# Routing a mixture of experts on one Trainium2 core: scatters by slot, or a token list made by matmuls and gathers

## The chip, the cores and the metric

The kernel runs on one core of a Trainium2 chip. The metric is device time in microseconds (us), the median of several executions. In the profile PE is TensorE (PEld its weight loads), DVE is VectorE, ACT is ScalarE, POOL is GpSimdE and SP is SyncE, which here only issues DMAs.

## The reference, cut to what matters

Two layers act on x, 32 batches of 128 tokens of 128 values (4096 tokens). Each layer is a cross attention with 16 heads over a context, then a mixture of 8 experts. All results are added to x with a tanh gate. The text calls them layer 1 and layer 2; the code has `layer == 0` and `layer == 1`.

```python
x = x + tanh(g_xattn[0]) * xattn0(layernorm(x), ctx)
x = x + tanh(g_ffn[0])   * ffn0(layernorm(x))
x = x + tanh(g_xattn[1]) * xattn1(layernorm(x), ctx)
x = x + tanh(g_ffn[1])   * ffn1(layernorm(x))

def ffn0(x):   # 8 experts, width 256, each expert picks its cap = 4096 / 8 = 512 best tokens
    probs = softmax(xt @ Wg)
    top_idx = top_k(probs.T, cap)                  # per expert
    masked = where(selected, probs.T, -inf)
    tok2exp = where(assigned, argmax(masked), argmax(probs.T))   # one expert a token
    return probs[tok2exp] * (gelu(x @ W1[tok2exp]) @ W2[tok2exp])

def ffn1(x):   # 8 experts, width 512, each token picks its two best, weights normalised to 1
```

## The kernel before, in words

Each layer has two stages. The **attention stage** (`pair_slots`) walks over 16 pairs of batches in software-pipelined slots: in slot p statistics are taken of pair p+4, it is transposed and projected as p+3, its queries and keys are written to DRAM and read back in another layout by SP (p+3, p+2), row maxima are found as p+1, scores and exponentials as p, values and output as p-1 and p-2. At the end, pair p-2 gets the statistics of the norm before the experts, and as p-3 its normed rows go to N and its router logits to LG. GpSimdE makes each reciprocal root (L445, L446 for the attention's norm, L466 to L469 for the experts'). Slots run from p = -4, so that the first pairs' statistics stand at the very start of the stage. The order of the work is written by hand, engine by engine, and each engine executes its own list in order.

The **expert stage** of layer 1 begins on DVE (`expert_layer`, L1210). `route_by_experts` (L1162) finds for each expert the 512th largest probability by a search on the bits of the float. It has ROUNDS = 15 rounds of BITS = 2 bits. A round (L1172 to L1184) counts for each of three candidates how many of 256 values per partition are at or above it (L1174, three counts with an accumulator), lets a matmul with SAME sum the counts over the partitions (L808), compares with 512, and takes the largest candidate that passed as the prefix of the next three. Then masks, two rank steps (`ranks`, L1087) and a choice of the best expert give each token a slot: expert e has a region of its own in DRAM, and the token takes the next free row of it (`slot_of`, L1096; `fill` adds the token's number and weight to its row of N).

GpSimdE scatters N to the DRAM tensor `dispatched` by 32 indirect DMAs, one for each batch (`dispatch`, L478; L494). Meanwhile DVE makes the tables of the tiles (`tables`, L1102): which rows and which expert each of TILES = 23 tiles of 256 slots has. SP waits for all scatters and reads the tiles, three buffers deep (L379 on). For each tile TensorE transposes it (L640), multiplies with the first matrices (L834), ScalarE applies Gelu (L615), TensorE multiplies with the second (L844), DVE scales by the tokens' weights (L1262), and GpSimdE scatters the result to `returned` in token order by two indirect DMAs of 128 rows (L504). After the last scatter SP reads it all back in four parts (L406), and DVE adds each to x with the gate (`combine`, L1268), one part at the head of each of the first four slots of layer 2's attention (`first_layer_result`, L1282).

Layer 2 routes during its attention, in groups of batches (`choose`, L885), scatters both choices of each token from GpSimdE's slots, and then has 39 tiles in the same manner. That part of the kernel keeps its form.

## Time and profile before

| | us |
|---|---|
| median of 3 runs | 791.73 (791.7 to 794.16) |
| the profiled execution, its time | 792.8 |
| the profiled execution, its span in the trace | 791.0 |
| busy in the span: PE, PEld | 539.4, 435.0 |
| busy in the span: DVE, ACT, POOL | 506.0, 346.8, 309.4 |
| mean granted TensorE clock | 0.847 of full |

The span is the time from the first to the last instruction of the trace. The stages lie in it about so: attention of layer 1 to 215 us, search and routing to 270, scatters to 312, tiles to 383, attention of layer 2 to about 590, its tiles to the end. A share of busy time is a mean over these stages, so it doesn't say what bounds one of them. PEclk is the clock that TensorE was granted, where 1.0 is 2.4 GHz and 0.5 is 1.2 GHz.

### The profile page before, as it was taken

To read this page: it belongs to the slowest core of one execution; us is meant where nothing else is said; L and a number is where in the kernel's file an instruction comes from. 1 tells how busy PE (TensorE), PEld (TensorE's weight loads), DVE (VectorE), ACT (ScalarE), POOL (GpSimd) and SP (SyncE) were. 2 spreads that over 40 slices of the span, in tenths; PEclk is the share of its full clock that TensorE was granted. 3 is DMA by queue.
4 is the path that set the end of the run, shared out by engine and by line. 5 is a ranking of instruction groups with operands and counts; after the bars stand their busy time and mean duration, and the time that the engine had idled before them with its cause. 6 is when DMAs were issued, how large, how long until landed. Compare 5 with 4: busy or idle time off the path is not lost.

```text
span 791.0 us, 17073 instructions
## 1 busy us (share of the span) xinstructions
PE 539.4 (68%) x5502; PEld 435.0 (55%) x5502; DVE 506.0 (64%) x1666; ACT 346.8 (44%) x798; POOL 309.4 (39%) x438
## 2 busy tenths in 40 slices
PE   1689999998511000988179999898710999999950
PEld 0467777776300000777156666675410899999940
DVE  4679888986287800344278999998662456655625
ACT  0256777777400000433026777675710555555510
POOL 6212233311200275477311224564775254554540
PEclk9979999999755555899559999999955899999985
DMA  8553332320000032233434555442113222222219
GB/s 270 149 179 97 97 93 85 92 83 4 1 0 0 18 106 62 75 108 101 129 115 144 167 161 162 138 131 76 37 49 107 59 72 76 73 72 72 69 56 297
DMA packets 97703, 76.71 MB, mean 97 GB/s; under 512 B 12880, under 2 KB 91600, under 8 KB 97168
## 3 DMA queue, kind: packets, MB, share of 16 engines
q1 hardware_dynamic: 89504, 57.27, 25.6%
q0 software_dynamic: 7040, 14.63, 5.5%
q10 hardware_dynamic: 1072, 3.73, 1.4%
q8 instruction: 46, 0.75, 0.4%
q14 instruction: 41, 0.34, 0.1%
HBM read 45.76 MB, written 33.62 MB: 100 GB/s over the span
## 4 chain that ended last, share of the span: by engine, by line
PE 46%; DVE 17%; issue 10%; POOL 9%; DMA 7%; ACT 5%; SPq 4%; ACTq 1%; DVEq 0%; POOLq 0%
PE bank L834 9%; PE bank L844 9%; PE bank L640 6%; PE bank L666 5%; PE bank L787 5%; POOL dispatched L479 4%; PE bank L654 4%; POOL returned L504 4%; DVE MX L979 4%; DVE PT L1174 2%; ACT OT L588 2%; PE bank L711 1%; PE bank L742 1%; PE bank L713 1%; PE bank L700 1%
## 5 line engine op out<-in xcount | busy, mean ns | idle before, releaser
L533 ACT ACTIVATE PT<-bank 128x512 f32<-128x512 f32 x256 | 151.9, 597 | 92.3 <-PE bank L654 91.5
L979 DVE TENSOR_REDUCE MX<-bank 128x4 f32<-128x512 f32 x256 | 172.8, 681 | 28.3 <-PE bank L666 26.1
L504 POOL DMA_INDIRECT returned<-PT,META_ROW x124 | 118.9, 959 | 113.4 <-DVE PT L1262 89.1
L479 POOL DMA_INDIRECT dispatched<-N,SLOT x96 | 94.7, 986 | 97.5 <-DVE EX L1217 57.4
L666 PE MATMUL bank<-KS,QS_N 96*128 96x128 f16 x1024 | 104.2, 227 | 11.7 <-DMA KS<-spread 7.2
L610 ACT ACTIVATE XGT<-bank 128x256 f32<-128x256 f32 x62 | 23.8, 383 | 191.7 <-PE bank L640 191.7
L844 PEld LDWEIGHTS bank<-WALL,HT 128*128 128x128 f32 x808 | 100.7, 195 | 7.3 <-issue 4.1
L844 PE MATMUL bank<-WALL,HT 128*128 x808 | 102.6, 279 | 1.6 <-ACT HT L615 0.8
L834 PE MATMUL bank<-XGT,XT_HL_WR 128*128 128x256 f32 x404 | 102.4, 394 | 0.0
L654 PE MATMUL bank<-QS_N,KS 98*128 98x512 f16 x256 | 98.1, 389 | 3.3 <-DMA QS_N<-MH 3.2
L666 PEld LDWEIGHTS bank<-KS,QS_N 96*128 96x128 f16 x1024 | 77.5, 103 | 35.9 <-DMA KS<-spread 9.4
L640 PE MATMUL bank<-CONST,PT 128*128 128x128 f32 x124 | 26.3, 296 | 82.8 <-issue 76.1
L834 PEld LDWEIGHTS bank<-XGT,XT_HL_WR 128*128 128x128 f32 x404 | 75.2, 199 | 8.0
L621 ACT ACTIVATE HT<-bank,XT_HL_WR 128x256 f32<-128x256 f32 x156 | 63.9, 471 | 21.4 <-PE bank L834 21.4
L787 PE MATMUL bank<-PT,VA 128*32 128x128 f32 x2048 | 70.6, 280 | 0.1
L640 PEld LDWEIGHTS bank<-CONST,PT 128*128 128x128 f32 x124 | 15.7, 151 | 87.3 <-issue 77.0
L787 PEld LDWEIGHTS bank<-PT,VA 128*32 128x32 f32 x2048 | 53.1, 111 | 18.0 <-issue 11.0
L466 POOL TENSOR_SCALAR MINUS<-MV_N 128x2 f32<-128x2 f32 x32 | 7.5, 233 | 127.4 <-DVE MV_N L883 127.2
L1258 DVE TENSOR_TENSOR PT<-bank,WALL 128x256 f32<-128x256 f32 x39 | 16.6, 425 | 43.9 <-PE bank L844 36.0
L1232 DVE COPY XT_HL_WR<-WALL 128x516 f32 (+1 forms) x62 | 23.7, 382 | 29.9 <-issue 19.6
L445 POOL TENSOR_SCALAR VE<-MV 128x2 f32<-128x2 f32 x32 | 7.0, 220 | 88.8 <-DVE MV L883 88.6
L1239 DVE CAST META_ROW<-PT 128x2 int32<-128x2 f32 x23 | 4.1, 177 | 56.9 <-DMA PT<-dispatched 35.5
(198 smaller groups left out, 890.5 us busy)
## 6 DMA issues: line engine op xcount, KB each, us to landing
spread<-XT_HL_WR SPq DMA_DIRECT2D x96, 128.0 KB
PT<-dispatched SPq DMA_DIRECT2D x62, 132.0 KB, 2.1
QS_N<-spread SPq DMA_DIRECT2D x128, 48.0 KB
KS<-spread SPq DMA_DIRECT2D x32, 192.0 KB
WALL<-in_w SPq DMA_DIRECT2D x8, 578.0 KB
CT<-in_ctx SPq DMA_DIRECT2D x32, 128.0 KB, 3.0
dispatched<-in_pads SPq DMA_DIRECT2D x2, 1056.0 KB
dispatched<-in_pads SPq DMA_DIRECT2D x16, 132.0 KB
```

Of the source, the lines that this page charges most:

```text
L479: pool.indirect_dma_start(xs[layer][:, :], bass.IndirectOffsetOnAxis(ap=SLOT[:, k, b:b + 1], axis=0), N[:, b, :], None).then_inc(scattered ...
L504: pool.indirect_dma_start(ys[layer][:, :], bass.IndirectOffsetOnAxis(ap=META_ROW[:, a.f, c:c + 1], axis=0), YS[:, a.f, c, :], None).then_i ...
L533: nc.scalar.activation(PT[:, c, 4 * g:4 * g + 4, :].rearrange("p j q -> p (j q)"), ST[i % 2][:, :], ACT.Exp, scale=SCALE[layer]).then_inc( ...
L610: nc.scalar.activation(XGT[:, a.u, :], bank[4 + a.u][:, 0:TILE], ACT.Copy).then_inc(xg_kept, 1)
L621: last = nc.scalar.activation(HT[:, a.u, m, :], bank[2 * a.u + m // 2][:, TILE * (m % 2):TILE * (m % 2) + TILE], ACT.Gelu, bias=WR[:, a.t, ...
L640: return nc.tensor.transpose(to, of, ident[0:n, 0:n])
L654: nc.tensor.matmul(ST[i % 2][:, :].rearrange("p (j q) -> p j q", j=J), KS[0:98, x.r, g, c * P:(c + 1) * P], QS[0:98, x.r, J * g:J * g + J, ...
L666: last = nc.tensor.matmul(MB[i % 2][:, j * P:(j + 1) * P], QS[0:96, m.r, J * g + j, c * P:(c + 1) * P], KS[0:96, m.r, g, c * P:(c + 1) * P ...
L787: last = nc.tensor.matmul(PA[32 * g:32 * g + 32, 256 * c + P * (j // 2):256 * c + P * (j // 2) + P], VA[:, b.r, c, head(g, j), :], PT[:, c ...
L834: last = nc.tensor.matmul(bank[2 * a.u + m // 2][:, TILE * (m % 2):TILE * (m % 2) + TILE], WR[:, a.t, m * P:(m + 1) * P], XGT[:, a.u, :], ...
L844: last = nc.tensor.matmul(bank[6 + a.u][:, c * D:(c + 1) * D], HT[:, a.u, m, c * P:(c + 1) * P], WALL[:, bass.ds(r + (W1COLS[layer] + m * ...
L979: V.tensor_reduce(out=MX[:, m.u, 2 * J * g + c:2 * J * (g + 1):2], in_=MB[i % 2][:, :].rearrange("p (j k) -> p j k", j=J), op=ALU.max, axi ...
```

## The change

**Search.** The candidates become whole numbers held as floats: the bits of the probabilities are cut to their high 14 bits for 8 rounds, then to the low 16 for 7 rounds. DVE makes two of the three counts and ScalarE the third, as a sum of signs, whose limit is 2 * 512 - 4096. The number of candidates that pass (an accumulator) times a step, plus a part worked out beforehand (PRE), gives the next three.

**Token list.** A slot is now a place in the row of all tiles (expert's first tile * 256 + rank), so that slot s lies in block s / 128 at place s % 128. OWN (128 tokens x 32 batches x 46 blocks) marks each token's block, POS its place. IDS is OWN times the token's partition (ScalarE) and OWN times its batch (GpSimdE). 32 matmuls of POS with IDS sum the partition and the batch of the token at each place of each block: LIST. The normed rows were stored plainly to DRAM (`normed`) by SP during the attention, and GpSimdE gathers two blocks for each tile, 46 gathers, in place of the 32 scatters and SP's reads.

**Results.** They aren't weighted and stay in slot order: DVE copies them, SP stores each tile plainly. In layer 2's attention GpSimdE gathers each batch's 128 rows by SLOT, 32 gathers, and DVE adds them to x with weight * gate (W0) for each pair before its statistics. The four combines are gone. Half of the tables, the tokens' numbers and weights in their rows, and some masking operations go; `starts` (the tiles' starts) now stands before the slots.

```diff
@@ route_by_experts, DVE
-                for t in range(ROUNDS):
-                    for m in range(CANDS):
-                        last = V.tensor_scalar(out=HITS[:, m, :], in0=PRT[:, :], scalar1=CAND[:, m:m + 1].bitcast(F32),
+                bits = PF[:, 0:B * E].bitcast(I32)
+                link(V.tensor_scalar(out=BITS_I[:, :], in0=bits, scalar1=((1 << 30) - 1) ^ low_mask, scalar2=None, op0=ALU.bitwise_and))
+                V.tensor_copy(PRT[:, :], BITS_I[:, :]).then_inc(candidates, 1)
+                dve.wait_ge(candidates, 2)
+                for t in range(ROUNDS):
+                    for m in range(CANDS - 1):
+                        last = V.tensor_scalar(out=HITS[:, m, :], in0=PRT[:, :], scalar1=CAND[:, m:m + 1],
                                                scalar2=None, op0=ALU.is_ge, op1=ALU.add, accum_out=COUNT[:, m:m + 1])
                     last.then_inc(mask_ready, 1)
+                    link(V.scalar_tensor_tensor(out=PRE[:, :], in0=sign, scalar=CAND[:, 0:1], in1=delta[:, t, :], op0=ALU.mult, op1=ALU.add))
+                    if t == 0:
+                        V.tensor_scalar(out=LOW_I[:, :], in0=bits, scalar1=low_mask, scalar2=None, op0=ALU.bitwise_and).then_inc(lows_cut, 1)
                     dve.wait_ge(counted, t + 2)
-                    link(V.scalar_tensor_tensor(out=BEST[:, 0:CANDS], in0=PO[:, 0:CANDS], scalar=float(CAP),
-                                                in1=CAND[:, :].bitcast(F32), op0=ALU.is_ge, op1=ALU.mult))
-                    if t < ROUNDS - 1:
-                        reduce(best, BEST[:, :], ALU.max)
-                        tt(CAND[:, :], best.bitcast(I32).broadcast_to([P, CANDS]), digit[:, t + 1, :], ALU.bitwise_or)
+                    link(V.scalar_tensor_tensor(out=PASSED[:, :], in0=PO[:, 0:CANDS], scalar=1.0, in1=limit, op0=ALU.mult, op1=ALU.is_ge,
+                                                accum_out=NPASS[:, :]))
+                    found = V.scalar_tensor_tensor(out=CAND[:, :], in0=step[:, t, :], scalar=NPASS[:, :], in1=PRE[:, :],
+                                                   op0=ALU.mult, op1=ALU.add)
...
@@ expert_layer, ScalarE
+                    for t in range(ROUNDS):
+                        act.wait_ge(candidates, t + 2)
+                        act.wait_ge(counted, t + 1)
+                        nc.scalar.activation(HITS[:, CANDS - 1, :], PRT[:, :], ACT.Sign, bias=CAND[:, CANDS - 1:CANDS],
+                                             accum_out=COUNT[:, CANDS - 1:CANDS]).then_inc(counted_act, 1)
...
+                    act.wait_ge(own, 1)
+                    nc.scalar.activation(IDS[:, :, 0, :], OWN[:, :, :], ACT.Copy, scale=const("partition")).then_inc(ids_p, 1)
@@ list_tokens, DVE (new)
+                V.tensor_tensor(out=OWN[:, :, :], in0=const("blocks").unsqueeze(1).broadcast_to([P, B, BLOCKS]),
+                                in1=sm[4].unsqueeze(2).broadcast_to([P, B, BLOCKS]), op=ALU.is_equal).then_inc(own, 1)
+                for k in range(4):
+                    V.tensor_tensor(out=POS[:, part * k:part * (k + 1), :], in0=const("places").unsqueeze(1).broadcast_to([P, part, P]),
+                                    in1=sm[5][:, part * k:part * (k + 1)].unsqueeze(2).broadcast_to([P, part, P]),
+                                    op=ALU.is_equal).then_inc(positions, 1)
...
+                dve.wait_ge(listed, 1)
+                link(V.tensor_copy(FIRST_IDS[:, :], PA[:, 0:BLOCKS]))
+                V.scalar_tensor_tensor(out=LIST[:, :], in0=PA[:, BLOCKS:2 * BLOCKS], scalar=float(P), in1=FIRST_IDS[:, :],
+                                       op0=ALU.mult, op1=ALU.add).then_inc(list_ready, 1)
@@ expert_layer, TensorE
+                    pe.wait_ge(ids_p, 1)
+                    pe.wait_ge(ids_b, 1)
+                    for b in range(B):
+                        if b % (B // 4) == 0:
+                            pe.wait_ge(positions, 4 * b // B + 1)
+                        last = nc.tensor.matmul(PA[:, 0:2 * BLOCKS], POS[:, b, :], IDS[:, b, :, :].rearrange("p k n -> p (k n)"),
+                                                start=(b == 0), stop=(b == B - 1))
@@ GpSimdE
-                if layer == 0:
-                    pool.wait_ge(copied, 1)
-                    for b in range(B):
-                        dispatch(0, 0, b)
+            def first_experts():
+                pool.wait_ge(own, 1)
+                nc.gpsimd.tensor_tensor(out=IDS[:, :, 1, :], in0=OWN[:, :, :], in1=const("batch").unsqueeze(2).broadcast_to([P, B, BLOCKS]),
+                                        op=ALU.mult).then_inc(ids_b, 1)
+                pool.wait_ge(normed_kept, 16 * PAIRS)
+                pool.wait_ge(list_ready, 1)
+                for i in range(TILES[0]):
+                    a = Tile(0, i)
+                    if a.g >= 3:
+                        pool.wait_ge(xg_t, a.g - 2)
+                    for c in range(2):
+                        pool.indirect_dma_start(XG[:, a.t, c, 0:D], None, normed[:, :],
+                                                bass.IndirectOffsetOnAxis(ap=LIST[:, 2 * i + c:2 * i + c + 1], axis=0)).then_inc(XA[a.t], 16)
+                for r in range(4):
+                    pool.wait_ge(SO[r], 16 * len(range(r, TILES[0], 4)))
+                gather_results(Pair(1, 0, 0))
@@ attention_slot, GpSimdE, after RSTD of pair p + 4
+                    if layer == 1:
+                        for k in range(2 * p + 9, min(2 * p + 11, PAIRS)):
+                            gather_results(Pair(1, k // 4, k % 4))
+            def gather_results(g):
+                if g.p >= 8:
+                    pool.wait_ge(combined, g.p - 7)
+                for c in range(2):
+                    pool.indirect_dma_start(YG[:, g.p % 8, c, :], None, ys[0][:, :],
+                                            bass.IndirectOffsetOnAxis(ap=SLOT[:, 0, g.b + c:g.b + c + 1], axis=0)).then_inc(YGS[g.p % 8], 16)
@@ attention_slot, SP, at the end of a slot (y = pair p - 3)
+                if (y := pair(-3)) and y.g < PAIRS:
+                    sp.wait_ge(n_copied, y.g + 1)
+                    sp.dma_start(normed[y.b * P:(y.b + 2) * P, :].rearrange("(c p) d -> p c d", p=P),
+                                 N[:, y.b:y.b + 2, 0:D]).then_inc(normed_kept, 16)
@@ attention_slot, DVE, before the statistics of n = pair p + 4
+                    if n and layer == 1:
+                        dve.wait_ge(YGS[n.p % 8], 32 * (n.p // 8 + 1))
+                        for c in range(2):
+                            last = V.scalar_tensor_tensor(out=batch(n, c), in0=YG[:, n.p % 8, c, :], scalar=W0[:, n.b + c:n.b + c + 1],
+                                                          in1=batch(n, c), op0=ALU.mult, op1=ALU.add)
+                        last.then_inc(combined, 1)
```

At digit 8 (`t + 1 == HIGH`) DVE also keeps the high digits, adds the low bits to what is left of the values, and loads the low candidates: a copy, a scaled sum over 256 values, a copy. The constants grow from 905 to 1214 columns of 128 values, since the tables of the search and of the list are among them.

## Rows read from the trace of the kernel before

**Rows 1.** Shares of the chain that ended last, whole kernel, by engine (page, part 4).
```profile
PE 46%; DVE 17%; issue 10%; POOL 9%; DMA 7%; ACT 5%; SPq 4%; ACTq 1%; DVEq 0%; POOLq 0%
```

**Rows 2.** Stretch 270 to 300 us: length, busy of PE, PEld, DVE, ACT, POOL, PEclk, DMA share, GB/s.
```profile
270.00:300.00 30.00, 0.00 (x0) 0.00 (x0) 6.59 (x27) 0.00 (x0) 22.99 (x24) 0.50 0.29 88
```

**Rows 3.** Timeline, from the search's end to the first scatter: start us, us, engine, line, operation.
```profile
252.46 0.61 DVE L1065 TENSOR_TENSOR RA<-PR,THR 128x256 f32<-128x256 f32 x1
...
268.36 0.18 DVE L1100 CAST SLOT<-SM 128x32 int32<-128x32 f32 x1
...
269.73 1.22 POOL L479 DMA_INDIRECT dispatched<-N,SLOT  x1 [57.45 <-DVE EX L1217]
```

**Rows 4.** The first stage's last scatter in the chain of waits: start us, us to landing.
```profile
309.22 2.26 DMA dispatched<-N,SLOT
```

**Rows 5.** Timeline of TensorE's work on tiles: three rows at 1.2 GHz, two at 2.4 GHz.
```profile
314.46 0.66 PE L640 MATMUL bank<-CONST,PT 128*128 128x128 f32 x2 [49.51 <-issue]
...
316.01 1.92 PE L834 MATMUL bank<-XGT,XT_HL_WR 128*128 128x256 f32 x4
...
320.89 2.07 PE L844 MATMUL bank<-WALL,HT 128*128 x8 [0.83 <-ACT HT L615]
...
329.64 1.03 PE L834 MATMUL bank<-XGT,XT_HL_WR 128*128 128x256 f32 x4
...
330.50 1.05 PE L844 MATMUL bank<-WALL,HT 128*128 x8
```

**Rows 6.** GpSimdE in 323.8 to 384.3 us, groups by line: busy us, mean ns, idle before.
```profile
L504 POOL DMA_INDIRECT returned<-PT,META_ROW x46 | 44.3, 962 | 28.5 <-DVE PT L1262 16.3 <-issue 12.2
```

**Rows 7.** Timeline of the end of the first expert stage and the start of layer 2.
```profile
377.81 0.61 DVE L1262 TENSOR_SCALAR PT<-bank,META_W 128x128 f32<-128x128 f32 x2 [1.20 <-PE bank L844]
...
389.89 0.29 DVE L880 BATCH_NORM_STATS2 STATS<-X 128x6 f32<-128x128 f32 x1
...
391.05 0.72 POOL L446 TENSOR_TENSOR RSTD<-VE,EXPO 128x2 f32<-128x2 f32 x1
...
393.64 0.29 DVE L880 BATCH_NORM_STATS2 STATS<-X 128x6 f32<-128x128 f32 x1
...
396.07 0.68 DVE L1029 TENSOR_TENSOR XT_HL_WR<-bank,XT_HL_WR 128x512 f16<-128x512 f32 x1
...
399.88 0.60 DVE L1014 TENSOR_SCALAR XN<-X,MV,RSTD 128x128 f32<-128x128 f32 x2 [1.13 <-POOL RSTD L446]
```

**Rows 8.** One 9 us slot of layer 2's attention, columns as in rows 2.
```profile
464.00:473.00 9.00, 8.56 (x121) 6.43 (x120) 8.75 (x30) 6.71 (x16) 2.28 (x6) 1.00 0.60 172
```

**Rows 9.** Timeline of one round of the search, and the start of the next.
```profile
221.96 0.48 DVE L1174 TENSOR_SCALAR_CACHE_REDUCE PT<-PT,CAND 128x256 f32<-128x256 f32 x1
...
223.16 0.09 DVE L1174 DVE_READ_ACCUMULATOR PT<-PT,CAND 128x1 bf16 x1
...
223.53 0.16 DVE L1178 SCALAR_TENSOR_TENSOR BEST<-bank,CAND 128x3 f32<-128x3 f32 x1 [0.28 <-PE bank L808]
...
224.11 0.48 DVE L1174 TENSOR_SCALAR_CACHE_REDUCE PT<-PT,CAND 128x256 f32<-128x256 f32 x1
```

**Rows 10.** Timeline: ScalarE's pass over 256 values, the Exp before the search.
```profile
216.59 0.42 ACT L604 ACTIVATE PR<-PR 128x256 f32<-128x256 f32 x1 [0.94 <-DVE PR L1150]
```

**Rows 11.** Timeline: ScalarE's change of function table in the first expert stage.
```profile
318.01 1.28 ACT L615 ACT_TABLE_LOAD   x1 [1.37 <-PE bank L834]
```

**Rows 12.** DVE over 256 values, groups by line with shapes, 214 to 270 us.
```profile
L1065 DVE TENSOR_TENSOR RK<-RK,bank 128x256 f32<-128x256 f32 x4 | 1.7, 421 | 0.1
```

**Rows 13.** GpSimdE's sum over 256 values, one line's instructions: ns least/median/most.
```profile
L451 POOL TENSOR_TENSOR X<-X,BIAS x16: 721/723/731, 18.1 to 156.0; 128x256 f32<-128x256 f32 x16
```

**Rows 14.** Four 128-column matmuls at the low clock, in the chain of waits.
```profile
403.13 0.61 PE bank L666 x4
```

**Rows 15.** DVE's scaled sum over 256 values, groups by line, 396 to 600 us.
```profile
L1042 DVE SCALAR_TENSOR_TENSOR X<-OK,GATES,X 128x256 f32<-128x256 f32 x16 | 7.6, 477 | 0.0
```

**Rows 16.** DMA issues by line: KB each, us from issue to landing.
```profile
CONST<-in_const SPq DMA_DIRECT2D x1, 452.5 KB, 3.4
```

More of the change, by code:

```diff
@@ L39, with search_tables @@
 CANDS = 2 ** BITS - 1
+HIGH = 8
 ROUNDS = 30 // BITS
+LOW_BITS = BITS * (ROUNDS - HIGH)
 GROUPS = ((0, 3), (3, 3), (6, 3), (9, 3), (12, 2), (14, 2))
 NB = 6
+def search_tables():
+    sign = np.ones(CANDS)
+    sign[-1] = -1
+    digit, step = np.zeros((ROUNDS + 2, CANDS)), np.zeros((ROUNDS, CANDS))
+    first, delta = np.zeros((2, CANDS)), np.zeros((ROUNDS, CANDS))
+    for phase, (t0, t1, unit) in enumerate(((0, HIGH, 2 ** LOW_BITS), (HIGH, ROUNDS, 1))):
+        half = np.zeros(CANDS)
+        half[-1] = unit / 2
+        here = [unit * 4.0 ** (t1 - 1 - t) * np.arange(1, CANDS + 1) - half for t in range(t0, t1)] + [np.zeros(CANDS)]
+        first[phase] = sign * here[0]
+        for t in range(t0, t1):
+            step[t] = sign * unit * 4.0 ** (t1 - 1 - t)
+            delta[t] = sign * (here[t - t0 + 1] - here[t - t0][0])
+    limit = np.full(CANDS, float(CAP))
+    limit[-1] = 2 * CAP - T
+    return sign, limit, first, step, delta
 def constants():
+    sign, limit, first, step, delta = search_tables()
     p = np.arange(P)[:, None]
@@ L63, in constants @@
         ("place", 2 * p + np.arange(2)[None, :]),
+        ("places", one * np.arange(P)[None, :]),
+        ("blocks", one * np.arange(BLOCKS)[None, :]),
+        ("batch", one * np.arange(B)[None, :]),
+        ("partition", one * p),
+        ("search_sign", one * sign),
+        ("search_limit", one * limit),
+        ("search_first", one * first.reshape(1, -1)),
+        ("search_step", one * step.reshape(1, -1)),
+        ("search_delta", one * delta.reshape(1, -1)),
     ]
@@ L389, in expert_layer @@
-                for i in range(TILES[layer]):
-                    a = Tile(layer, i)
-                    if a.g >= 3:
-                        sp.wait_ge(xg_t, a.g - 2)
-                        sp.wait_ge(meta, a.g - 2)
+                sp.wait_ge(pads, 16 * (1 + E))
+                sp.wait_ge(scattered, 16 * B * 2)
+                for i in range(TILES[1]):
+                    a = Tile(1, i)
+                    sp.wait_ge(xg_t, a.g - 2)
+                    sp.wait_ge(meta, before(i - 2))
@@ new lines, in slot @@
+                        link(V.tensor_tensor(out=w2, in0=is_second, in1=row[:, :, D + 2], op=ALU.mult))
+                        V.tensor_tensor(out=META_W[:, a.f, :], in0=w1, in1=w2, op=ALU.add).then_inc(meta, 1)
+                    if (a := tile(-1)) and layer == 0:
+                        dve.wait_ge(y_done, a.g + 1)
+                        await_results(dve, a)
+                        V.tensor_copy(YS[:, a.f, :, :].rearrange("p c d -> p (c d)"), bank[6 + a.u][:, 0:2 * D]).then_inc(y_kept, 1)
@@ new lines, in slot @@
+                    if (a := tile(-1)) and layer == 1:
+                        dve.wait_ge(y_done, a.g + 1)
+                        dve.wait_ge(meta, a.i + 1)
+                        y = bank[6 + a.u][:, 0:2 * D].rearrange("p (c d) -> p c d", c=2)
+                        r = dve.value_load(TBL[0:1, 1, a.i:a.i + 1], min_val=0, max_val=(E - 1) * W)
+                        link(V.tensor_tensor(out=YS[:, a.f, :, :], in0=y,
+                                             in1=WALL[:, bass.ds(r + (W - D), D)].unsqueeze(1).broadcast_to([P, 2, D]), op=ALU.add))
```

323 lines of the change are left out of this document (174 added, 149 removed).

## The prediction

> **What bounds the kernel now.** The view to read first is the chain of waits, because the kernel is a series of stages and each has another limit. Over the whole kernel TensorE holds 46% of the chain, but DVE has 17% and GpSimdE 9% [rows 1], and the diff touches stages where these two decide. Next comes the table of stretches. From 270 to 300 us TensorE executes nothing and GpSimdE is busy for 22.99 of 30 us [rows 2]: this is the dispatch, 32 scatters in a line. The timeline gives its ends. The first operation after the search starts at 252.46, the slots are ready at 268.54, and the first scatter starts at 269.73 [rows 3]. The last starts at 309.22 and lands 2.26 us later [rows 4], and the first token tile reaches TensorE at 314.46 [rows 5]. Then the 23 tiles run at GpSimdE's pace: 46 scatters of 962 ns, with 0.30 us between two [rows 6], make 2.53 us a tile. TensorE at 2.4 GHz needs only 1.03 + 1.05 and about 0.4 for the transposes, 2.5 in sum but overlapped [rows 5]. The last result is scaled at 378.42, yet the statistics of layer 2 start at 389.89 [rows 7], because the scatter backlog, its landing, a read back and a combine lie between. In layer 2's attention one 9 us slot holds 8.75 us of DVE and 8.56 of TensorE work, and 2.28 of GpSimdE [rows 8].
>
> **The change, term by term.** The sum is made against the profiled execution, whose span is 791.0 us.
>
> *Search, -6.0 us.* A round lasts 2.15 us (221.96 to 224.11). It has three counts on DVE (1.29 us to the end of the last accumulator read), 0.28 of TensorE and its semaphores, and then three small operations of 0.16 with 0.03 between [rows 9]. After the change DVE makes two counts (1.29 less one pitch of 0.40: 0.89), TensorE keeps 0.28, and two small operations remain, the first with an accumulator read of the kind that takes 0.09: 0.16 + 0.09 + 0.16 and three gaps, 0.45. That is 1.62, or 0.53 saved, 8.0 over 15 rounds. The operation for PRE lies beside TensorE. ScalarE's count runs beside the two DVE counts. No row shows a ScalarE count with a sum; its nearest row is a plain pass over 256 values, 416 ns [rows 10]. Bounds are that 0.42 and twice a DVE count with its read, 1.1. I take 0.6, near the row, so it is covered by the 0.89. Against the 8.0 stand whole-number steps that are new: a mask and a cast before round 0 instead of one copy (+0.4), the low bits cut in round 0 (+0.35), the change from high to low digits (a copy, a scaled sum over 256 values, a copy, +0.85), and three small ones at the end (+0.4). Net -6.0, range -8.5 to +1.
>
> *A possible table load, 0.* ScalarE's change from Exp to Gelu shows a 1.28 us load after 1.37 idle [rows 11]; whether Sign needs one no row shows. Exp ends at 217.01 [rows 10] and the first round began 2.15 before 221.96, at 219.81 [rows 9]: 2.8 us in which a load can hide. Its bound is once 2.65. The Trainium skill, "ScalarE: Activation LUTs" (What ACT_TABLE_LOAD costs), has 1.28 us plus a drain of 1.38 for every switch to another set, which agrees with that row. By this rule, with the load behind the wait, the sum would be 2.65 us worse.
>
> *Routing after the search, -1.7 us.* It takes 15.9 us from 252.46 to the slots. An operation over 256 values takes 0.42 to 0.61, a small one 0.18 [rows 3, 12]. Removed: threshold copy 0.2, two casts of the mask 0.6, in each of two rank steps a copy and a subtraction (1.3), and of the masking a small one and two over 256 values (1.0): 3.1, each priced between these rows. Added: five to seven small operations for the tile starts, which stood behind the first scatter before, +1.4. Bounds -2.5 and -0.5.
>
> *Token list in place of the scatters, -30.6 us.* Before, 45.9 us lie between slots and first transposes (268.54 to 314.46). New, after the slots: three small operations 0.63; OWN over 1472 values, 1.75 by one value per 1.04 ns as the 256 in 0.42 imply [rows 12]. GpSimdE then multiplies 1472 values: 723 ns for 256 [rows 13] makes 3.3 (if 0.2 of it is start) to 4.2. DVE makes POS in the meantime (4 x 1.2 = 4.8), and 32 matmuls of 92 columns follow. Four of 128 columns took 0.61 with the clock low [rows 14], so 0.15 each, 4.8. GpSimdE's 3.4, then 4.8 and a gap: 8.3, bounds 6 and 11. Two reads of the bank 0.45, GpSimdE's wake 0.3. The list stands at slots + 11.4. Two gathers are issued (the second 1.5 later) and land: 2.3 as the scatter did [rows 4], bounds 1.8 and 4.2. First transposes at slots + 15.3.
>
> The port is a place where a rule speaks against the change. The GpSimdE sums of [rows 13] lie between 721 and 731 ns in all 16, so nothing held them up there. The Trainium skill, "SBUF — State Buffer" (SBUF: two separate sides), says that DVE with two SBUF inputs and GpSimdE exclude each other for a whole instruction. POS has two such inputs; by this rule its last quarter would end 3.2 us later and the list 0.7 later, the sum -35.5.
>
> *Tile stage, -1.7 us.* It lasts 64.0 us from first transposes to 378.42. New: GpSimdE issues 46 gathers instead of 46 scatters, each for the price of [rows 6], 44 steps x 1.265 = 55.7 from the first tile's rows to the last's, then a tile's way to its result, 6.35 as for the last tile before, and 0.3 for buffers in the cold start. 62.3. No row shows a gather's issue; the scatter's 0.96 is the nearest, both bounds 0.8 and 1.15, so -9 to +8 us for the stage. SP's stores are issued beside it.
>
> *Return, -4.7 us.* Before 11.5 us from 378.42 to 389.89. New: a store and its landing 2.3, wake 0.3, second gather's start 1.3, landing 2.3, two scaled sums of 0.3: 6.8. Bounds -6 and -1.
>
> *Front of layer 2, +3.5 us.* The new gathers stand between two pairs' reciprocal roots on GpSimdE, four to a slot, 5.05 us. In time from the first statistics (389.89), RSTD ends at 1.9 [rows 7]. The second pair's gathers land at 5.8, its statistics run at 6.4 instead of 3.75, and the low halves that DVE writes behind it (L1029) at 8.9 instead of 6.2: +2.7 for the first maxima. Pair three: RSTD is queued behind gathers until 13.5, XN at 14.5 instead of 10.0 [rows 7]. Part of that is hidden by slots that soon last 9 us [rows 8], longer than 5.05 + 0.9. Taken +3.5, bounds +2 and +8. The four old combines of 1.3 on DVE go.
>
> *DVE in layer 2, +4.5 us.* Twelve more pairs get two scaled sums over 128 values. One over 256 takes 477 ns [rows 15], so with their wait 0.55 a pair. While TensorE is the nearer limit part is hidden; with DVE at 8.75 of 9 [rows 8] all counts: half of six and all of six is 5.0, taken 4.5, bounds 2 and 6.6.
>
> *Start, +0.5 us.* The constants grow from 905 to 1214 columns, 154 KB more before anything may start; 452.5 KB landed in 3.4 us beside other loads [rows 16], so 0.5, bounds 0 and 1.2. SP gets 16 stores of N in layer 1's attention: issued at each slot's end, before SP waits for the next maxima in any case. 0, or +2 if their 2 MB slow the others.
>
> Sum -6.0 - 1.7 - 30.6 - 1.7 - 4.7 + 3.5 + 4.5 + 0.5 = -36.2. The profiled run took 792.8, that becomes 756.6; the median of the three runs is 1.07 lower, 791.73, so 755.5. Forecast 756.
>
> **Rivals.** *ScalarE's count is the longer branch.* For it: no row of a ScalarE sum. Against it: 0.42 against 0.89. If the pass takes 1.4, the rounds keep their 2.15 and 8 us are lost: 764. *Layer 2 pays double.* Gathers and roots share GpSimdE, 2 MB more are in flight where slots wait for DMAs, and every DVE operation counts: +16 instead of +8: 764. *Gathers land late.* Buffers are three, so a landing over about 5.5 us sets the pace. A scatter landed in 2.26 [rows 4], and the slowest landing in my rows is 3.4, the constants' among other loads [rows 16]. At 7 us a tile takes 3.0, +11, and each single gather's way costs 4.7 more, in list, return and front: 781.
>
> *TensorE stays at 1.2 GHz, and the kernel is slower.* Place: tile stage. TensorE idles before it and granted clock was 0.50 [rows 2]; at that clock a tile takes 0.66 + 1.92 + 2.07 = 4.65 [rows 5] against 2.53. Before, it rose between the rows of 320.89 and 329.64, with a backlog of landed rows; now rows come one tile at a time. For 23 tiles +48.8, so 805. It decides from 17 tiles on. Against it: at 1.2 GHz a tile needs longer than the feed gives, so TensorE is then never idle, and that went before the rise.
>
> *It doesn't do what it says*: only if the gathers had to wait for the 16 stores of N, and the search and 15.9 us of routing lie between. No chance of its own.
>
> **Chances.** Forecast 0.66 (own range 745 to 766), ScalarE 0.11, layer 2 double 0.12, late landing 0.06, low clock 0.05. The range 745 to 772 leaves out the last two and tails of the first. A change of 0.3% (2.4 us) is about what a measurement of this kernel can tell. Only the low clock isn't faster: faster 0.94, same 0.01, slower 0.05.
>
> **What would show it.** Rounds of 1.6 us with ScalarE's count ended before DVE's; 11.4 us from slots to list and 15.3 to the first transposes; 46 gathers at 1.26 in a line, none waiting for TensorE; 6.8 us from last result to statistics; third pair's XN 14.5 after the first statistics; DVE without idle time in layer 2. I am wrong if the tile stage isn't at GpSimdE's pace or if the front loses over 8 us.

## The result, and the profile after

The changed kernel takes 761.6 us (median of 4 runs, 757.79 to 766.54), the kernel before 791.72 beside it (4 runs, 790.95 to 794.16). The ratio is 0.962, with a 95% interval of 0.956 to 0.968: 30.1 us less. The forecast was 756 in a range of 745 to 772.

The profiled executions are 760.45 us (span 758.6) and 792.8 (span 791.0), 32.4 us apart. First, the chain that ended last by engine, which answers to [rows 1].

```profile
PE 41%; DVE 22%; issue 11%; POOL 10%; DMA 8%; ACT 5%; SPq 2%; ACTq 1%; POOLq 0%; DVEq 0%
```

DVE's share went from 17% to 22%, and GpSimdE's from 9% to 10% only, because it now has gathers on the path where it had scatters. The stretch of [rows 2], of the changed kernel, has the list's matmuls on TensorE up to 273.7 us and the tiles' from 279 on (columns as there):

```profile
270.00:300.00 30.00, 19.64 (x117) 16.22 (x115) 11.29 (x31) 8.02 (x16) 19.10 (x20) 0.67 0.27 59
```

The timeline gives where each stage begins, in both traces by the same marks (the forecast's value stands beside them). The columns are us.

| stage, by its marks | before | after | change | forecast |
|---|---|---|---|---|
| start and attention of layer 1, up to the router's first operation | 215.7 | 217.2 | +1.5 | +0.5 |
| search, to the first mask | 36.8 | 31.8 | -5.0 | -6.0 |
| routing, to the slots | 16.1 | 14.4 | -1.6 | -1.7 |
| slots to the first transposes | 45.9 | 15.8 | -30.1 | -30.6 |
| tiles, to the last result | 64.0 | 66.2 | +2.2 | -1.7 |
| return, to the first statistics of layer 2 | 11.5 | 7.2 | -4.3 | -4.7 |
| front, to the first maxima | 14.0 | 17.5 | +3.5 | +3.5 |
| layer 2's attention, first to last maxima | 153.1 | 154.4 | +1.2 | +4.5 |
| the rest | 234.0 | 234.2 | +0.2 | 0 |

The changes add up to -32.4, as the spans do. One round of the search and the start of the next (timeline, start us, us), to be held against [rows 9]:

```profile
223.46 0.51 ACT L698 ACTIVATE PT<-PT,CAND 128x256 f32<-128x256 f32 x1
223.46 0.48 DVE L1285 TENSOR_SCALAR_CACHE_REDUCE PT<-PT,CAND 128x256 f32<-128x256 f32 x1
...
223.88 0.19 ACT L698 ACTIVATION_READ_ACCUMULATOR PT<-PT,CAND 128x1 bf16 x1
224.27 0.09 DVE L1285 DVE_READ_ACCUMULATOR PT<-PT,CAND 128x1 bf16 x1
224.27 0.22 DVE L1288 SCALAR_TENSOR_TENSOR PRE<-CONST,CAND 128x3 f32<-128x3 f32 x1
...
224.71 0.16 DVE L1292 SCALAR_TENSOR_TENSOR PASSED<-bank,CONST 128x3 f32<-128x3 f32 x1 [0.23 <-PE bank L909]
...
224.92 0.22 DVE L1294 SCALAR_TENSOR_TENSOR CAND<-CONST,NPASS,PRE 128x3 f32<-128x3 f32 x1
225.17 0.48 DVE L1285 TENSOR_SCALAR_CACHE_REDUCE PT<-PT,CAND 128x256 f32<-128x256 f32 x1
```

A round takes 1.71 us (223.46 to 225.17). ScalarE's count with its accumulator read ends 0.61 after the start (224.07), DVE's second with its read at 0.90 (224.36). So ScalarE is the shorter branch.

From the slots (263.46) to the first gather, the chain of waits (start us, us, what):

```profile
264.16 1.69 DVE PT L1340
265.85 6.99 DVE HT L1344 x4
...
272.89 0.81 PE bank L922 x8
...
274.03 0.22 DVE LIST L1350
...
275.11 1.23 POOL PT L582
...
276.64 0.95 POOL PT L582
```

The chain goes through POS (L1344): its four parts take 6.99 us, and behind the last of them stand 8 matmuls of 0.10. GpSimdE's product is not in the chain, but it made one of the parts long, as an experiment below shows. LIST is ready at 274.24, 10.8 after the slots, and the first gather starts 11.65 after them. The end of the stage, in the chain of waits:

```profile
329.66 0.95 POOL PT L582
...
330.91 0.95 POOL PT L582
...
332.16 7.04 DMA PT<-normed,LIST
...
339.25 0.44 PE bank L740 x2
...
345.43 1.82 DMA returned<-PT
...
349.33 2.59 DMA HT<-returned,SLOT
```

Gathers follow each other every 1.25 us, but the last one lands 7.04 us after its start, where the one of the first tile took 2.60 (276.64 to 279.24).

### The profile page after: what moved, and what is told of

It is laid out like the page before. It is cut to its first block, busy times and chain, and to the rows that moved or that the text cites. A ratio compares the mean times of both kernels' runs of the same rounds, so it can differ in the third digit from the quotient of the medians.

```text
span 758.6 us, 16969 instructions
## 1 busy us (share of the span) xinstructions
PE 539.6 (71%) x5534; PEld 435.7 (57%) x5534; DVE 502.7 (66%) x1605; ACT 358.3 (47%) x830; POOL 315.0 (42%) x439
## 4 chain that ended last, share of the span: by engine, by line
PE 41%; DVE 22%; issue 11%; POOL 10%; DMA 8%; ACT 5%; SPq 2%; ACTq 1%; POOLq 0%; DVEq 0%
PE bank L943 10%; PE bank L953 10%; DVE MX L1089 7%; PE bank L740 5%; POOL PT L582 5%; PE bank L766 4%; PE bank L887 4%; PE bank L754 3%; POOL dispatched L556 3%; DVE PT L1285 2%; DMA PT<-normed,LIST 2%; PE bank L842 1%; ACT XT_HL_WR L654 1%; DMA QS_N<-MH 1%; ACT OT L678 1%
## 5 line engine op out<-in xcount | busy, mean ns | idle before, releaser
L593 POOL DMA_INDIRECT returned<-PT,META_ROW x78 | 74.9, 961 | 84.6 <-DVE PT L1403 72.4
L556 POOL DMA_INDIRECT dispatched<-N,SLOT x64 | 64.3, 1004 | 30.0 <-issue 14.1
L721 ACT ACTIVATE HT<-bank,XT_HL_WR 128x256 f32<-128x256 f32 x156 | 64.0, 471 | 21.4 <-PE bank L943 21.4
L582 POOL DMA_INDIRECT PT<-normed,LIST x46 | 43.8, 953 | 19.8 <-issue 13.1
L552 POOL DMA_INDIRECT HT<-returned,SLOT x32 | 31.8, 993 | 23.5 <-DMA returned<-PT 15.0
```

The costliest lines, as they stand in the source:

```text
L556: pool.indirect_dma_start(xs[:, :], bass.IndirectOffsetOnAxis(ap=SLOT[:, k, b:b + 1], axis=0), N[:, b, :], None).then_inc(scattered, 16)
L582: pool.indirect_dma_start(XG[:, a.t, c, 0:D], None, normed[:, :], bass.IndirectOffsetOnAxis(ap=LIST[:, 2 * i + c:2 * i + c + 1], axis=0)). ...
L593: pool.indirect_dma_start(ys[1][:, :], bass.IndirectOffsetOnAxis(ap=META_ROW[:, a.f, c:c + 1], axis=0), YS[:, a.f, c, :], None).then_inc(S ...
L721: last = nc.scalar.activation(HT[:, a.u, m, :], bank[2 * a.u + m // 2][:, TILE * (m % 2):TILE * (m % 2) + TILE], ACT.Gelu, bias=WR[:, a.t, ...
```

## The experiments

Eleven runs follow, of nine variants: the changed kernel ran once more, and one variant twice. Each was timed beside the kernel before, on one of three chips. On the first the kernel before took 792.6 us, about as above. The second and third are slower, by some 5% for that kernel (833.4 and 831.6); there the comparison is by ratio, or between kernels that ran together on one chip.

**Where the gathers read.** The list has 46 x 128 = 5888 places, and 4096 tokens. Each of the 1792 empty places gives row 0 of `normed`, and they are dense at the end: by the reference's own data, tiles 21 and 22 are all empty and tile 20 has 8 tokens. The experiment gives an empty place a row of its own, with the same 46 gathers. The partition number is made one larger, so that an empty place reads 0, and two small operations set `filler` there. Its control has the same operations and sends all empty places to row 0.

```diff
-        ("partition", one * p),
+        ("partition", one * (p + 1)),
+        ("filler", one * (np.arange(BLOCKS)[None, :] % B * P + 1) + p),      # control: one * np.ones((1, BLOCKS))
@@ list_tokens
+                link(V.scalar_tensor_tensor(out=FILL[:, :], in0=TOKF[:, :], scalar=0.5, in1=const("filler"), op0=ALU.is_lt, op1=ALU.mult))
+                V.scalar_tensor_tensor(out=LIST[:, :], in0=FILL[:, :], scalar=-1.0, in1=TOKF[:, :], op0=ALU.add, op1=ALU.add)
```

> Edit: the places of the token list that hold no token point to distinct rows of the normed tensor instead of all to row 0; two more small DVE operations make it. In the changed kernel the first tile stage took 66.2 us from its first transposes to its last result, 3.9 more than my sum, and the last gather landed 7.0 us after its issue, where the first took 2.4. Theory A, row 0 is a hot spot (1792 of the 5888 places are empty, and the last six gathers read hardly anything else): all gathers land in 2.3 to 3 us, the stage falls to 60 to 62 us, the run to 5 us less than the same kernel with all empty places on one row, and the runs spread less. Rival B, the landing grows because gathers, stores and matmul fetches share the DMA engines: landing stays at 5 to 7 us for the last, stage 66, time the same within 1 us.

> Edit: the same two more DVE operations as in the run before, but the filler is 1 at every empty place, so that all of them still read row 0. It is the control. Theory A and rival B both expect the changed kernel's time plus 0.4 to 0.5 us for the two operations: 761 to 763, tile stage 66, last landing about 7.

Measured: spread 755.02 us, ratio 0.9552 (0.9519 to 0.9586); control 758.93, ratio 0.9583 (0.9557 to 0.9609). The intervals of the ratios overlap, but the two ran together and their medians are 3.9 us apart: five of the six spread runs are below the fastest of the control (757.64). Theory A had 5 us, and runs that spread less; they didn't (752.82 to 760.94, the control's 757.64 to 761.47). The control was expected at 761 to 763 and came 2.7 below the changed kernel, which does less, so medians scatter by that much and the time alone would be thin evidence. The tile stage, by the profiled runs, is 61.1 against 64.6, with 66.2 in the changed kernel. What ties this to the empty places are stretches near the end of the stage. First the changed kernel (columns: length, busy of PE, PEld, DVE, ACT, POOL, PEclk, DMA share, GB/s):

```profile
325.00:332.00 7.00, 5.16 (x37) 4.46 (x36) 2.19 (x6) 2.56 (x5) 5.33 (x6) 1.00 0.84 105
332.00:339.00 7.00, 4.25 (x28) 3.63 (x27) 1.14 (x3) 1.96 (x4) 0.95 (x1) 1.00 0.81 59
```

The first of them with the empty places spread:

```profile
325.00:332.00 7.00, 6.01 (x41) 5.20 (x40) 2.28 (x6) 2.58 (x6) 4.72 (x5) 1.00 0.36 98
```

And the control, whose gathers run 2.7 us later:

```profile
332.00:339.00 7.00, 5.17 (x35) 4.47 (x35) 1.63 (x4) 2.31 (x5) 2.83 (x3) 1.00 0.97 63
```

The queue of the gathers alone (packets, MB, share of the 16 DMA engines) shows whose time it is: changed kernel 325 to 332, spread 325 to 332, control 332 to 339.

```profile
q0 software_dynamic: 144, 0.33, 63.5%
```

```profile
q0 software_dynamic: 180, 0.39, 21.4%
```

```profile
q0 software_dynamic: 137, 0.31, 90.6%
```

With the rows spread, more packets of this queue take a third of the time. The gathers are the same 46 and the operations the same as in the control, so it is the reads of one row that take longer. The landings say it by size too. In the trace of the next experiment, which has all 46 of them and leaves the empty places on row 0, the four blocks before the end that are empty throughout landed after 3.6, 3.7, 3.9 and 3.6 us and the full blocks after 2.6 in the median; the last six, one behind the other with hardly a token, took 3.6 rising to 5.8. In the spread kernel the last two gathers with a recorded landing (of 128 empty places each) took 2.4. In the control the last gather lands after 5.85 us; in the spread kernel the chain reaches the stage's end by another way:

```profile
322.57 3.56 DMA PT<-normed,LIST
...
326.18 0.44 PE bank L743 x2
326.62 0.87 PE bank L946 x4
327.48 1.12 PE bank L956 x8
328.61 0.22 PE bank L743 x2
```

From 326.2 to the last result TensorE works with a single gap (0.59 us), so its 2 us a tile end the stage, not the landing of the last gathers. Single gathers in the middle land late for another reason, which isn't known: the one issued at 304.94 in the spread kernel took 4.66 us, and the one at 306.67 in the changed kernel 5.37, though its block is full of tokens.

**DVE counts alone.** ScalarE's count goes back to DVE, and the rest of the new search stays.

```diff
-                    for m in range(CANDS - 1):
+                    for m in range(CANDS):
@@ ScalarE: its counts and the wait for them go; the third candidate is a plain one (sign, half and limit not special)
```

> Edit: the third count goes back to DVE as a count like the other two, ScalarE's signs are gone; everything else of the changed search stays. Theory: ScalarE's count and its accumulator read end at 0.61 us of the 0.81 that DVE's two counts take, so it was free, and a third DVE count adds its pitch of 0.40 to each of 15 rounds: rounds of 2.11 instead of 1.71, +6.0 us. Rival: the round is bound by the chain over TensorE and its semaphores, which a count could hide beside: less than +2.

Measured: 766.06 us, ratio 0.9668 (0.9635 to 0.9701), 4.5 over the median of the changed kernel. The search takes 38.16 us instead of 31.79, 6.4 more where 6.0 were expected, and a round 2.12, a part of which follows (start us, us).

```profile
250.58 0.48 DVE L1277 TENSOR_SCALAR_CACHE_REDUCE PT<-PT,CAND 128x256 f32<-128x256 f32 x1
...
252.44 0.22 DVE L1286 SCALAR_TENSOR_TENSOR CAND<-CONST,NPASS,PRE 128x3 f32<-128x3 f32 x1
252.70 0.48 DVE L1277 TENSOR_SCALAR_CACHE_REDUCE PT<-PT,CAND 128x256 f32<-128x256 f32 x1
```

So whole numbers gain next to nothing in a round (2.12 against 2.15), and with the steps around them they cost 1.4 us (38.16 against 36.78). ScalarE's count alone brings 6.4 us, of which the search keeps 5.0.

**Gathers of layer 2 one pair ahead.** GpSimdE issues two gathers in a slot, not four, and two pairs before the first slot.

```diff
                 gather_results(Pair(1, 0, 0))
+                gather_results(Pair(1, 0, 1))
@@ attention_slot
-                        for k in range(2 * p + 9, min(2 * p + 11, PAIRS)):
+                        for k in range(p + 6, min(p + 7, PAIRS)):
```

> Edit: GpSimdE gathers layer 1's results of the first two pairs before layer 2's first statistics, and then one pair a slot instead of two. Theory: the front of layer 2 lost 3.5 us (17.5 from first statistics to first maxima where 14.0 were) because the second pair's gathers were issued behind the first root and the third root behind four gathers. Then the second statistics come 4 to 4.5 us after the first instead of 6.8, XN of the third pair 10.5 instead of 14.9, the first maxima at 14 to 15, and the run is 2.5 to 3.5 us shorter than the changed kernel. Rival: the front is bound by the DMA round trips of queries and keys: first maxima still at 17, time the same.

Measured: 758.5 us, ratio 0.9586 (0.9554 to 0.9619), 3.1 under the changed kernel's median, but not told apart from it by the ratios. By the profile the front is 14.6 us, not 17.5. GpSimdE's rows, first of the changed kernel, then of this one, show how:

```profile
353.76 0.73 POOL L513 TENSOR_TENSOR RSTD<-VE,EXPO 128x2 f32<-128x2 f32 x1
...
360.54 0.72 POOL L513 TENSOR_TENSOR RSTD<-VE,EXPO 128x2 f32<-128x2 f32 x1
361.45 1.08 POOL L552 DMA_INDIRECT HT<-returned,SLOT  x1 [0.19 <-issue]
362.83 1.07 POOL L552 DMA_INDIRECT HT<-returned,SLOT  x1 [0.30 <-issue]
364.21 0.95 POOL L552 DMA_INDIRECT HT<-returned,SLOT  x1 [0.30 <-issue]
365.46 0.95 POOL L552 DMA_INDIRECT HT<-returned,SLOT  x1 [0.30 <-issue]
366.76 0.72 POOL L513 TENSOR_TENSOR RSTD<-VE,EXPO 128x2 f32<-128x2 f32 x1
```

```profile
350.30 0.72 POOL L513 TENSOR_TENSOR RSTD<-VE,EXPO 128x2 f32<-128x2 f32 x1
...
353.96 0.72 POOL L513 TENSOR_TENSOR RSTD<-VE,EXPO 128x2 f32<-128x2 f32 x1
...
357.70 0.72 POOL L513 TENSOR_TENSOR RSTD<-VE,EXPO 128x2 f32<-128x2 f32 x1
```

The third root comes 13.0 us after the first where the gathers lie between, and 7.4 where they don't. But layer 2's attention took 155.9 us in this run, 1.6 more than in the changed kernel. Whether that is the gain given back is the question of a later run.

**The second chip.** The changed kernel again, beside three variants.

> Edit: none, the changed kernel once more, beside its variants. Its four runs lay between 757.8 and 766.5, wider than those of before. If the chip's runs scatter by place of the DRAM tensors, the median of these five falls in 758 to 763; both theories of the tile stage expect its last landing at 5 to 7 us and the stage at 64 to 66.

Measured: 802.7 us against 833.37, ratio 0.9639 (0.9607 to 0.9671). My range of times was wrong since the chip is another; the ratio is the same within its interval. The last gather landed after 5.91 us, inside the 5 to 7 expected, but the tile stage took 75.0 us where I expected 64 to 66. Against the first trace the tiles take 8.8 us more, layer 2's attention 19.7 and the rest 12.4, while search, routing, list and return are equal within 0.1. The waits of this stretch name, for the engines of the tile stage, a releaser that no instruction of this trace is (285 to 345 us: line, releaser, us in total, times, longest):

```profile
DVE PT L1394 <- remote: 15.4, 5, 4.7
ACT XGT L710 <- remote: 11.7, 5, 3.8
```

What holds the engines on these chips was not found. The ratio of the two kernels, measured on this chip and in the result, doesn't show it (0.964 and 0.962).

**No sums.** The scaled sums of pairs 5 to 16 of layer 2 are left out, so x lacks layer 1's experts there; gathers, waits and signals stay.

```diff
+                            if n.p < 4:
                                 last = V.scalar_tensor_tensor(out=batch(n, c), in0=YG[:, n.p % 8, c, :], ...
-                        last.then_inc(combined, 1)
+                        last.then_inc(combined, 1) if n.p < 4 else dve.sem_inc(combined, 1)
```

> Edit: the scaled sums that add layer 1's results to x are left out for pairs 4 to 15, with gathers and waits kept (so layer 2 works on a partial x there). I had priced them at 4.5 us; from the first to the last maxima the changed kernel takes only 1.2 us more than before, 154.35 against 153.11. Theory A: DVE had idle time in these slots, and about 7 us of sums fill it: leaving them out saves 1 to 2.5 us. Rival B: every DVE operation counts and something else in the slots became shorter: it saves 6 to 7.

Measured: 803.09 us, ratio 0.9624 (0.9583 to 0.9665), against 802.7 with the sums on the same chip. The attention lasts 171.2 against 174.1 us, a difference inside what the variants of one chip show (1 to 3 us) and not seen in the median, so neither the 1 to 2.5 us of theory A nor the 6 to 7 of rival B show in the time. The sums are 24 x 0.33 = 8 us of DVE's time and next to nothing of the kernel's. DVE's busy time over 160 us from the first maxima, before and after (columns as above), shows where they went:

```profile
403.90:563.90 160.00, 143.94 (x1918) 105.55 (x1915) 147.00 (x421) 107.43 (x237) 64.46 (x113) 0.96 0.44 130
```

```profile
370.10:530.10 160.00, 141.31 (x1904) 103.56 (x1902) 152.22 (x443) 106.46 (x235) 83.97 (x132) 0.97 0.48 139
```

DVE was idle for 13.0 of 160 us before, and is for 7.8 now: 5.2 of the new work went into idle time. The slot of [rows 8], with 8.75 of 9 us busy, was fuller than the mean.

**Batch product on DVE.** GpSimdE's product (L573) moves to DVE, ahead of POS.

```diff
-                nc.gpsimd.tensor_tensor(out=IDS[:, :, 1, :], in0=OWN[:, :, :], in1=const("batch")..., op=ALU.mult)
+                V.tensor_tensor(out=IDS[:, :, 1, :], in0=OWN[:, :, :], in1=const("batch")..., op=ALU.mult)
```

> Edit: OWN times the batch is made by DVE, before POS, instead of by GpSimdE beside it. In the changed kernel the first quarter of POS ends at 269.4, 3.6 us after its start, where the others take 1.13, and GpSimdE's multiplication lies exactly in it (265.93 to 269.48). Theory A, the two exclude each other while both read two SBUF inputs: each quarter takes 1.13 to 1.2, DVE needs 1.7 for the product, and the list is ready at slots + 10.2 instead of 10.8. Rival B, the first quarter is slow by itself, for its waits or its strides: it stays 3.6 long, and the list comes at slots + 12.4.

Measured in a single run (800.44 us, so the time alone says nothing): slots to first transposes 15.01 us against 15.85 on the same chip, and the list 10.06 after the slots, where theory A had 10.2, though DVE has 1.69 us more to do. The four parts of POS, ns least/median/most, in the changed kernel and then here:

```profile
L1344 DVE TENSOR_TENSOR HT<-CONST,SM x4: 1210/1214/3659, 265.8 to 271.6; 128x1024 bf16<-128x1024 f32 x4
```

```profile
L1344 DVE TENSOR_TENSOR HT<-CONST,SM x4: 1218/1218/1219, 268.2 to 271.6; 128x1024 bf16<-128x1024 f32 x4
```

The GpSimdE product of the changed kernel is the first row, the long part of POS the second:

```profile
265.93 3.55 POOL L573 TENSOR_TENSOR PT<-PT,CONST 128x1472 bf16<-128x1472 bf16 x1 [52.10 <-DVE PT L1340]
...
266.90 3.66 DVE L1344 TENSOR_TENSOR HT<-CONST,SM 128x1024 bf16<-128x1024 f32 x1
```

The long part is the second of the four, where the expectation says the first. The first, from 265.77, took 1.22 us though GpSimdE's product began beside it, and the second ends 1.1 us after the product (269.48), about its own length. DVE stood still for 2.4 us. All nine traces with the product on GpSimdE, on all three chips, have this second part at 3659 to 3664 ns, and the three with it on DVE have none over 1219. The Trainium skill, "SBUF — State Buffer" (SBUF: two separate sides), says that a DVE operation with two SBUF inputs and a GpSimdE operation that reads SBUF exclude each other for the whole instruction; the traces agree.

**All four edits.** Spread places, one pair ahead, product on DVE, and 4 stores of 8 batches at the end of layer 1's attention instead of 16 of 2.

> Edit: four changes to the changed kernel together: distinct rows for the empty places; the multiplication by the batch on DVE in place of GpSimdE; one pair of results gathered a slot, two ahead; the 16 stores of the normed rows as 4 at the end of layer 1's attention. Theory: they touch different stages and add up: tiles -4 (61 instead of 64.6 to 66), list -0.6, front -2.9, attention of layer 1 0 to -1, less 0.5 for the filler: 7 to 9 us under the changed kernel in the same call, and under 754. Rival: what the front gains is given back in layer 2's attention, as the trace with one pair ahead hints (155.9 us instead of 154.4): then only 5 to 6 us.

Measured: 795.91 us, ratio 0.9546 (0.9514 to 0.9578): 6.8 us under the changed kernel on this chip, between what the two theories gave (7 to 9, and 5 to 6). List 15.5 us (its two added operations included), front 14.3, both as expected. But the tiles took 74.0, only 1.0 less than in the changed kernel here, where I expected 4: what holds the tile stage on this chip is mostly not the empty places. The sum was right in part by luck.

**The third chip: which of the edits count.** The changed kernel didn't run here. Two edits (spread places and one pair ahead); all four again; and the late stores alone:

```diff
-                if (y := pair(-3)) and y.g < PAIRS:
+                if (y := pair(-3)) and y.g < PAIRS and y.p % 4 == 3 and y.p > 11:
                     sp.wait_ge(n_copied, y.g + 1)
-                    sp.dma_start(normed[y.b * P:(y.b + 2) * P, :]...
+                    for k in range(4):
+                        sp.dma_start(normed[8 * k * P:(8 * k + 8) * P, :]...
```

> Spread empty places and gathers in layer 2 one pair ahead, nothing else. My theory is that the two are independent terms: tile stage 61.1 us as with the spreading alone, front 14.6 as with the later gathers alone, about 9 us under the changed kernel of the same call (ratio 0.951 to 0.953 to the kernel before). Rival: a front that starts sooner is given back in layer 2's attention (153.9 with spreading alone, 155.9 with the later gathers alone), so that only the spreading stays: ratio 0.955, and first to last maxima of layer 2 last 155.5 or more.

> All four edits again (spread empty places, gathers one pair ahead, batch product on DVE, 4 stores of N late in place of 16), beside its parts in the same call. If the terms add, it is the two edits' time less 0.8 us for the product (list in 15.0 us and two small operations more, 0.5) and nothing for the stores: within 1 us of the run with two edits. If the 16 stores cost layer 1's attention something, up to 2 us less, and then the run with late stores alone shows it too.

> Only the stores of N in layer 1's attention are moved: 4 of 8 batches at its end in place of 16 of 2 batches, one per slot. My forecast took 0 for them with a bound of 2 us. At 0: this is the changed kernel's time (ratio 0.962 within 0.003) with layer 1's attention at 160 to 162 us as in all variants. Rival: 2 us less (ratio 0.959) and attention below 159.5.

| | us, median of 6 | ratio to before (95%) | attention 1 | tiles | front | attention 2 |
|---|---|---|---|---|---|---|
| two edits | 793.49 | 0.9545 (0.9514 to 0.9576) | 161.2 | 71.3 | 14.3 | 170.6 |
| all four | 793.38 | 0.9564 (0.9528 to 0.9599) | 161.7 | 71.2 | 14.5 | 171.8 |
| late stores alone | 798.24 | 0.9581 (0.9548 to 0.9614) | 160.1 | 74.1 | 17.3 | 173.9 |

The product on DVE and the late stores bring nothing that these times show: two edits and four are equal. The ratio of the two edits, 0.9545, lies between what the sum of the terms gave (0.951 to 0.953) and the rival's 0.955; attention 2 is no test of the rival here, since its 155.5 us was meant for the first chip. The stores alone met neither expectation (ratio 0.962, or 0.959 with attention below 159.5): 0.9581 with attention at 160.1, and variants without them had 159.2 and 159.8. So whether the late stores bring something by themselves stays open. Between late stores and two edits lie 4.75 us in the medians, and the profiles give 2.8 to the tiles and 3.0 to the front (the profiled run of the two edits was their fastest, 788.79). Attention 2 isn't longer with the earlier front, so the 1.6 us of the run with one pair ahead were most likely its scatter, and the front's gain stays.

The best version is the one with two edits, or with spread places alone: the first has a ratio of 0.9545 on the third chip, the second 0.9552 on the first, against 0.962 and 0.964 of the changed kernel in its two comparisons. The intervals don't tell the two apart.

## Why the prediction was right, and where it wasn't

The forecast of 756 was 5.6 us low. The sum said -36.2, the profiled run -32.4. Two terms are most wrong, with opposite sign: +3.9 in the tile stage, -3.3 in layer 2's attention. That they nearly cancel is luck; without it the time would still lie in the range. The search and the start add 1.0 each, the list 0.5. The profiled run lies another 1.1 us under the median, where the one of the kernel before lay over it.

*List in place of the scatters: right* (-30.1 against -30.6), but its inner steps were off both ways. The matmuls cost 0.10 each, not 0.15: I had taken the price of 128 columns, with the last one's full length in it, for matmuls of 92. They ran in four groups of 8, each behind its part of POS, and ended 7.8 us after OWN, where I had 8.3. In turn GpSimdE's product (3.55, taken 3.4) held one part of POS for 2.4 us, as the port's rule had it. So the list stood at 10.8 us and the first gather at 11.65 after the slots, where I had 11.4 for both. Of the two sums that I gave, -36.2 and -35.5, the one with the rule was right in kind, but its 0.7 was not what it cost: with the product on DVE, which then has 1.69 us more to do, the list still came 0.7 us sooner.

*Tile stage: the term that was mis-sized.* My step "then a tile's way to its result, 6.35 as for the last tile before" took every gather to land like the first. The stage is 44 pitches, 332.16 - 276.64 = 55.5 (I had 55.7), plus the difference of two landings, 7.04 - 2.60 = 4.4, plus 6.2 from there to the result: 66.2. The price of an issue and the pace were right, the landing was not. I had read the landing off a scatter that writes 128 different rows [rows 4] and didn't ask which rows the last gathers read: the reference's data has 1792 empty places, and the diff gives them all the number 0. The rival "gathers land late" named 7 us, but for every gather; it holds for the last two alone (6.8 and 7.0 us). With three buffers a late one in between is absorbed: the gather at 306.67, landed after 5.37 us, held TensorE for 3.06 us and GpSimdE's gathers for some 0.5. The last of a stage never is.

*DVE in layer 2: mis-sized.* I took 4.5 from one slot with 0.25 us of slack; over 160 us DVE had 13 us, and 5.2 us of the work went there. The cost is 1.2 by the traces, and 0 by the run that leaves the sums out. That I should have read from one long stretch. The rival "layer 2 pays double" fell with it: front and attention cost 4.7 together, not 16.

*Search: off by 1.0.* The round is 1.71, not 1.62, and nearly all of it is the gap for TensorE, 0.35 rather than 0.28 (224.36 to 224.71). The two small operations take 0.46 with their gaps, as foreseen (0.45): the last is 0.22 instead of 0.16, but the accumulator's read lies inside the first. The saved time is (2.15 - 1.71) x 15 = 6.6, less 1.6 of added steps, where I had 8.0 less 2.0. ScalarE's count took 0.51 + 0.19 (0.61 in all), where I had taken 0.6: that rival fell. No table load stands between Exp and Sign; ScalarE's first load in the layer is Gelu's, as before.

*Routing, return, front: right.* Routing -1.6 (-1.7). Return 7.2 (6.8). In the front I had the second pair's statistics at 6.4 and its low halves at 8.9; they came at 6.8 (359.38) and 9.3 (361.88), and the third pair's XN at 14.9 instead of 14.5 (row below), all from the first statistics at 352.60.

```profile
367.52 0.60 DVE L1131 TENSOR_SCALAR XN<-X,MV,RSTD 128x128 f32<-128x128 f32 x2 [3.64 <-POOL RSTD L513]
```

*Start.* The first statistics come 0.5 us later, as forecast; the other 1.0 in that row of the table is scatter, since layer 1's attention lasted 159.2 to 162.5 us in kernels that have the same code there.

*TensorE stays at 1.2 GHz: fell.* The granted clock, 0.50 before, rises between 285 and 295 us and is 1.00 for the next ten. It fell once more in the stage, behind the late gather: TensorE was idle from 309.0 to 312.1, was granted 0.50 for some 3 us behind it, and 1.00 again from 317 on. The last of the rows holds that dip.

```profile
285.00:295.00 10.00, 9.69 (x54) 9.01 (x55) 2.53 (x7) 4.69 (x10) 7.56 (x9) 0.77 0.38 82
295.00:305.00 10.00, 9.16 (x65) 8.18 (x64) 3.25 (x9) 4.22 (x10) 7.56 (x9) 1.00 0.47 116
...
313.00:317.00 4.00, 4.00 (x18) 3.59 (x17) 0.72 (x2) 0.98 (x2) 2.88 (x4) 0.57 0.31 76
```

At the low clock a tile needs longer than its feed, so from 285.3 us on TensorE had no gap up to 295, and from the third tile's first matrices (289.6 us, 1.03 for four matmuls instead of 1.91) the clock was up.

## What to carry to other kernels

Price a gather by the rows that its indices name, those of padding and empty places above all: let them read different rows, or their landing at the end of a stage is paid in full (about 4 us here). Take the slack of an engine from a long stretch, not from one slot that looks full. A chain of work on one engine that others wait for is worth dividing between two engines even at a few tenths of a us per round, if the round repeats; and what is put between two short steps on GpSimdE's queue (here four gathers of 1.25 us) delays the second by all of it.

## What the runs showed of the hardware that was not expected

Gathers whose 128 places read one row of DRAM landed after up to 7.04 us, and 137 packets of their queue held 90.6% of the DMA engines' time over 7 us; with different rows 180 packets held 21.4%, and the landings recorded at the stage's end were 2.4. A DVE operation of 1214 ns took 3659 beside a GpSimdE operation of 3552, and the one before it, which had started first, took 1217. And chips differ: on two of three the kernel before took 5% longer (833 and 832 against 792 us); the changed kernel ran on one of these too, with a ratio of 0.964 against 0.962.
